# Reordering the written-out schedule of a mixture-of-experts and Mamba block on four engines

## The reference

```python
x = x + 0.5 * ffn(layernorm(x))        # 8 experts, hidden 512, top 2 of 8 by a softmax gate, silu
x = x + mixer(layernorm(x))            # two Mamba blocks in a row, the second followed by a chunked memory read
x = x + 0.5 * ffn(layernorm(x))        # the same expert weights again
```

## Time and profile before

| | us |
|---|---|
| median of 3 runs (1960.1 to 1960.5) | 1960.4 |
| the profiled execution's own time | 1957.77 |
| its span, first to last instruction | 1955.9 |
| VectorE busy | 1723.2 (88%) |
| TensorE busy | 1511.4 (77%) |
| ScalarE busy | 1142.5 (58%) |
| GpSimd busy | 755.6 (39%) |

### The profile page before, as it was taken

One profiled execution on the slowest core, in us unless ns is written; L12 is line 12 of the kernel. 1 busy time (PEld: TensorE's weight loads), 2 busy tenths in 40 slices (PEclk: granted clock), 3 DMA queues, 4 the chain that ended last, 5 costly groups with the idle time before them and its releaser, 6 DMA issues. The chain is left out here.

```text
span 1955.9 us, 26508 instructions
## 1 busy us (share of the span) xinstructions
PE 1511.4 (77%) x8672; PEld 1313.5 (67%) x8672; DVE 1723.2 (88%) x2421; ACT 1142.5 (58%) x2206; POOL 755.6 (39%) x366
## 2 busy tenths in 40 slices
PE   5778547878878787878888787887888888548778
PEld 4667435777767676767677667776777777437667
DVE  4269999999989998999989999899989999999941
ACT  3276555566756665656666566665755657436522
POOL 0005354444434354454325354353434454443310
PEclk9889767879989889998989898988889799668879
DMA  5000000000000000000000000000000000000000
GB/s 182 1 6 1 1 1 1 6 1 1 1 13 1 1 1 7 6 1 1 1 8 6 1 1 7 7 1 1 1 6 1 1 1 1 6 1 1 1 6 6
DMA packets 11688, 14.45 MB, mean 7 GB/s; under 512 B 400, under 2 KB 8592, under 8 KB 11408
## 3 DMA queue, kind: packets, MB, share of 16 engines
q1 hardware_dynamic: 11536, 12.56, 2.0%
HBM read 10.46 MB, written 2.10 MB: 6 GB/s over the span
## 5 line engine op out<-in xcount | busy, mean ns | idle before, releaser
L1101 POOL TENSOR_TENSOR acc<-acc,G 128x1024 f32<-128x1024 f32 x192 | 557.9, 2905 | 467.6 <-DVE G L922 461.4
L912 DVE TENSOR_TENSOR_SCAN hs<-dA,dbu 128x1024 f32<-128x1024 f32 x256 | 646.4, 2543 | 3.1 <-issue 2.2
L566 ACT ACTIVATE raw<-b_h 128x512 f32<-128x512 f32 x512 | 305.0, 598 | 340.7 <-PE b_h L328 324.8
L623 ACT ACTIVATE dA<-delta,A 128x255 f32<-128x255 f32 x1024 | 422.7, 495 | 55.3 <-DVE hs L912 35.8
L405 PE MATMUL b_r<-bcr,selr 128*128 128x256 f32 x1024 | 245.5, 343 | 199.8 <-DVE G L922 118.5
L405 PEld LDWEIGHTS b_r<-bcr,selr 128*128 128x128 f32 x1024 | 184.0, 217 | 249.3 <-DVE G L922 134.5
L922 DVE TENSOR_TENSOR G<-hs,b_r 128x1024 f32<-128x1024 f32 x256 | 309.9, 1211 | 9.6 <-issue 3.0
L902 DVE TENSOR_TENSOR dbu<-du,b_r 128x1024 f32<-128x1024 f32 x256 | 308.2, 1209 | 0.4
L326 PE MATMUL b_h<-xh,w1h 128*128 128x512 f32 x512 | 242.4, 473 | 83.7 <-DVE xa L838 27.9
L335 PE MATMUL b_h<-w2s,raw 128*128 128x128 f32 x2048 | 279.7, 292 | 0.0
L335 PEld LDWEIGHTS b_h<-w2s,raw 128*128 128x128 f32 x2048 | 269.3, 209 | 1.1
(11 more groups left out here) (144 smaller groups left out, 1652.8 us busy)
## 6 DMA issues: line engine op xcount, KB each, us to landing
xin<-x_dram SPq DMA_DIRECT2D x8, 256.0 KB, 2.9
raw<-w_dram SPq DMA_DIRECT2D x1, 2048.0 KB, 11.2
out_dram<-ob SPq DMA_DIRECT2D x8, 256.0 KB, 2.3
prm<-pack_dram SPq DMA_DIRECT2D x1, 1124.5 KB, 5.2
hs<-sel_dram SPq DMA_DIRECT2D x2, 512.0 KB, 12.4
G<-sel_dram SPq DMA_DIRECT2D x2, 512.0 KB, 7.6
dA<-early_dram SPq DMA_DIRECT2D x1, 512.0 KB, 11.5
dbu<-early_dram SPq DMA_DIRECT2D x1, 384.0 KB, 11.7
```

The lines of the kernel that those rows point to most:

```text
L566: do(hT[e % 2][:, c, :], H[i % 2][:, :], ACT.Silu).then_inc(f_hact, 1)
L623: last = do(dA[j % 4][:, d, k, 1:], delta[b][:, k, 1:], ACT.Exp, scale=A[:, k, s:s + 1])
L912: V.tensor_tensor_scan(flat(hs[j % 2]), flat(dA[j % 4]), flat(dbu[j % 2]), 0.0, ALU.mult, ALU.add)\
L1101: Q.tensor_tensor(acc[b][:, :, :, :], (G[0] if j == 1 else acc[b])[:, :, :, :], G[j % NG][:, :, :, :], ALU.add).then_inc(q_gs, 1)
```

## The change

The strings of `ORDER` are replaced by others; no other line is changed. The words of each string are the same as before but for two things that cross a slot's border: VectorE's f2 and f3 of the FFN in slots 2 and 3 move from slot 3 to slot 2, and two of TensorE's pieces move from slot 1 to slot 0 (33 and 31 pieces in place of 31 and 33; 24 and 40 in slots 2 and 3 stay).

```diff
@@ -44,39 +44,37 @@
 
 ORDER = {
     "tensor": (
-        "t0 t1 fturn in t2 fgate p2 t3 p2 t4 p5 t5 p2 t6 t7 xp p1 dt p2 t8 p1 t9 p2 t10 p3 m1 t11 p2 t12 "
-        "t13 p4 m2 p3 t14 m3 t15 p1 m4 p1",
-        "p2 t0 t1 t2 p5 out p6 turn t3 p1 t4 t5 in p2 t6 t7 p2 t8 t9 xp p1 t10 p2 t11 p1 t12 p1 dt p4 t13 "
-        "t14 p6 t15",
-        "t0 fturn t1 fgate p1 t2 p1 t3 out p4 t4 p5 turn t5 p2 t6 in t7 t8 p1 t9 p3 t10 xp p1 t11 p2 t12 p2 "
-        "t13 p2 dt t14 t15",
-        "p5 t0 p1 turng t1 p3 in t2 t3 t4 p8 t5 t6 xp p4 t7 t8 dt m1 p1 t9 t10 p3 t11 p1 m2 p2 t12 p2 t13 "
-        "t14 p2 m3 p5 t15 p3 m4"),
-
-
+        "t0 t1 t2 fturn in t3 fgate t4 p2 xp p4 t5 t6 p7 t7 dt t8 t9 p4 m1 t10 t11 p5 t12 p3 m2 p1 t13 p2 m3 p2 "
+        "t14 t15 p1 m4 p2",
+        "t0 p1 t1 p5 t2 p1 out t3 t4 p5 t5 turn t6 in p1 t7 p1 t8 p1 xp p1 t9 p1 dt t10 t11 p4 t12 p4 t13 p6 t14 "
+        "t15",
+        "fturn t0 t1 fgate p1 t2 t3 p3 out p5 t4 p2 t5 p2 turn t6 t7 in t8 p1 t9 p1 t10 p2 xp p1 t11 p4 dt p2 t12 "
+        "t13 t14 t15",
+        "p5 t0 p3 turng t1 p1 in p1 t2 p2 t3 t4 p4 xp p2 t5 t6 p1 t7 p1 dt p1 t8 p2 t9 p2 m1 t10 t11 t12 m2 p4 "
+        "t13 p4 t14 m3 p2 m4 p3 t15 p2",
+    ),
     "scalar": (
-        "d0 fhigh d1 d2 r xm F0 ftanh F1 d3 d4 proj d5 sp F2 F3 oT d6 v d7 rT",
-        "d0 d1 F4 F5 d2 turned d3 d4 d5 d6 r xm F6 proj F7 d7 sp",
-        "fhigh d0 d1 d2 F0 F1 ftanh d3 turned d4 d5 d6 d7 r xm F2 proj F3 sp",
-        "turned d0 d1 d2 F4 r xm F5 d3 proj d4 d5 d6 sp oT F6 v F7 rT d7"),
-
-
-
+        "d0 fhigh d1 d2 r xm F0 ftanh proj F1 d3 d4 d5 sp F2 oT F3 d6 v rT d7",
+        "d0 d1 F4 F5 d2 d3 turned d4 d5 d6 r xm d7 proj F6 F7 sp",
+        "d0 fhigh d1 d2 d3 F0 F1 d4 ftanh turned d5 d6 d7 r xm F2 proj F3 sp",
+        "d0 turned d1 d2 F4 r xm F5 proj d3 d4 d5 d6 d7 sp oT F6 F7 v rT",
+    ),
     "vector": (
-        "gate flow b0 flog ftop b1 s0 s1 g0 b2 g1 b3 s2 s3 fweights g2 b4 low f0 s4 f1 g3 b5 g4 s5 b6 g5 b7 "
-        "delta mask s6 g6 s7 g7 xb f2",
-        "f3 fstats gate b0 b1 s0 xsum s1 un g0 b2 g1 s2 f4 b3 fnorm s3 g2 f5 b4 g3 b5 s4 s5 g4 b6 g5 s6 b7 "
-        "low s7 g6 f6 f7 g7 delta",
-        "flow b0 flog gate s0 b1 g0 xsum ftop b2 un s1 s2 g1 b3 lx fweights s3 g2 b4 f0 g3 f1 s4 b5 g4 s5 "
-        "b6 g5 b7 s6 s7 ln low unx g6 delta g7",
-        "f2 b0 b1 f3 s0 gate g0 b2 s1 s2 fstats g1 b3 low g2 s3 b4 g3 f4 s4 f5 b5 g4 b6 delta mask s5 s6 g5 "
-        "b7 g6 s7 g7 f6 fnorm f7 xb"),
-
+        "b0 b1 gate flow s0 flog b2 ftop g0 s1 fweights s2 g1 b3 low g2 s3 f0 g3 b4 f1 b5 delta s4 s5 g4 b6 g5 "
+        "mask b7 f2 s6 s7 g6 g7 xb",
+        "f3 fstats b0 b1 gate s0 s1 xsum g0 g1 un b2 b3 f4 s2 s3 g2 b4 fnorm f5 g3 s4 b5 g4 s5 b6 g5 s6 b7 low f6 "
+        "delta s7 f7 g6 g7",
+        "flow b0 flog ftop b1 gate s0 s1 xsum g0 g1 b2 un b3 s2 s3 fweights g2 lx b4 g3 f0 f1 b5 s4 ln g4 s5 b6 "
+        "g5 b7 low unx s6 delta g6 s7 f2 g7 f3",
+        "b0 b1 s0 gate b2 g0 s1 s2 g1 low b3 g2 s3 g3 b4 b5 fstats f4 f5 s4 delta g4 s5 mask b6 g5 s6 b7 g6 s7 f6 "
+        "g7 fnorm xb f7",
+    ),
     "gpsimd": (
         "a1 a2 a3 a4 a5 a6 a7",
         "rms rs froot a1 a2 a3 a4 a5 a6 a7",
-        "rms a1 a2 rs lnx rmsx a3 a4 a5 a6 a7",
-        "a1 a2 a3 a4 froot a5 a6 a7"),
+        "rms rs a1 a2 lnx a3 rmsx a4 a5 a6 a7",
+        "a1 a2 a3 froot a4 a5 a6 a7",
+    ),
 }
```

## The result

The changed kernel takes **1828.0 us** (median of 4 runs, 1825.4 to 1829.5) against 1960.4 for the kernel before in the same comparison (1960.1 to 1961.6): ratio 0.932, 95% interval 0.931 to 0.934. The direction was right, the size was not. The profiled execution took 1825.4 us.

What follows compares the result with a forecast made beforehand. VectorE was taken as the bound; 11.6 us per group over six groups (69.6) plus 12 for groups 0 and 7 made 82 off 1957.8, giving 1876, and 1878 us as median. Range 1845 to 1930 us.

Steps and rivals of the forecast that it cites:

- The stock of 16.7 us per group: VectorE's time lost per group before the change, in scans, delta, du and xn held by GpSimd adds (meetings): 16.7 us.
- Meetings left, 7.2 per group: VectorE instructions still held by GpSimd adds in the new order: 0.1 + 2.0 + 2.6 + 2.5 us over four slots.
- The chain of fturn, in, fgate is as long as before, 9.3 us: Slot 0, TensorE: time from f7's end to the logits stays at 9.3 us.
- the wait that was to be 1.9: Slot 0: VectorE's wait for the logits shrinks from 4.9 to 1.9 us, 3.0 gained.
- TensorE's lateness, 1.8 per group: TensorE's B7 about 0.9 and f2 0.6 us late in slot 0, C7 0.3 in slot 3: 1.8 lost per group.
- Rival 1: TensorE falls behind in places, p6 10.9 us at half clock; gain 4 to 8 per group, about 1915 us; chance 0.21.
- rival 2: TensorE's clock falls through new waits and it becomes the bound, slower than before: 2050 us at worst; chance 0.09.
- Half the gain in groups 0 and 7: Groups 0 and 7, half their slots without FFN, gain half as much: 12 us for both.
- The cover of GpSimd's short steps: froot and rs move by one add on GpSimd; costed at nothing, the norm needing froot being ten words later.
- Rival 3: All meetings and waits go, TensorE never late: 14 to 15 us per group, about 1848 us; chance 0.08.

Runs made afterwards that it cites:

- before_filled_tensore: Kernel before, with two extra unused matmuls ahead of t0 and two ahead of fturn in TensorE's slot 0; 1954.7 us, ratio 0.995 to 0.998.
- after_old_gpsimd: Changed kernel with GpSimd's four old strings put back (rs, rmsx and froot differ in place, slots 2 and 3); 1839.8 us, against 1828.0.
- after_norms_moved_2: Changed kernel with VectorE's fnorm moved behind delta in slots 1 and 3, and slot 3 ending s7 g7 f6 xb f7; 1822.9 us, against 1828.0.

## Why the prediction was right in direction and wrong in size

**The mechanism holds.** VectorE bounds the kernel, its scans, delta, du and the words of the norms are held by GpSimd's adds, and how much is lost follows from the order. Small adds took 125 us from the kernel before with no order changed. The stock of 16.7 us per group was right within 1%.

**The bill by terms.** The forecast had 82 us, the spans differ by 132.4. From the runs with small adds, 92.7 of these are meetings (135.3 to 42.6): 71 in groups 1 to 6, where the forecast had 57, and 21 in groups 0 and 7, where it had about 10 of its 12. VectorE's rest fell by 29.5, where it had about 15; the waits for logits alone fell by 24.1 (40.5 to 16.4). The other 10.2 us of busy time (1587.9 to 1577.7) are in no term of the forecast; 3.3 of them are in un (10.9 to 7.6 with small adds) and 4.6 in inputs and products (618.7 to 614.1), the rest was not followed.

1. *Meetings left, 7.2 per group: too high.* A middle group has 5.2, by its busy time with full and with small adds: fnorm 1.2 in slot 1 and 2.1 in slot 3 (forecast 1.4 and 2.4), un 1.2 and unx 0.7 in slot 2 (1.4 and 0.9), un in slot 1 nothing (0.4), the scans 0.1 or less (0.7), du and delta none. So each norm word was high by 0.2 to 0.3, and the small meetings at s4 to s7 and at un in slot 1, counted by adding word to word from the slot's start, did not come. A scan directly behind a product goes first, and the add behind it waits; I had read that in rows 5 and still charged some of these.
2. *"The chain of fturn, in, fgate is as long as before, 9.3 us": wrong.* It takes 7.3 us in two groups, 8.2 in two and 9.2 in one, and the wait that was to be 1.9 is 0 to 1.8, 0.8 on average. I took durations from before for TensorE work that had run at the lower clock. before_filled_tensore shows the link of clock and length. Rows 7 held a sign of it: 3.69 us of idle ahead of fturn.
3. *TensorE's lateness, 1.8 per group: did not come.* In groups 2 to 5 inputs wait for spreads once per group, for 0.2 to 0.3 us; over the run it is 6.0 us, most of it in groups 0, 1 and 7, and the waits for expert sums (`ob` and `xa` for b_h, 19.4 before) are 18.4. I had let TensorE keep its old pace while VectorE got faster; its clock rose instead: it was 0.88 to 0.90 in the middle groups and is 0.93 to 0.95. Rival 1 stands on the same error, and rival 2 has the sign wrong. Rival 1's price was also read wrongly from rows 9: 16 matmuls of L335 are four downs and not two, so a down takes 0.49 or 0.91 us, and p6 takes 2.9 or 5.4 us, not 5.9 or 10.9.
4. *Half the gain in groups 0 and 7: too low.* By the ends of their last products they gained 9.4 us (with 1.6 from the start) and 15.1, 24.5 in place of 12. Groups 1 to 6 gained 108 in place of 69.6.
5. *The cover of GpSimd's short steps* was named only through the words that need their results. They also decide when adds run: 11.8 us in after_old_gpsimd.
6. *Rival 3 was added up wrongly*, and with it the low end. 14 to 15 per group is about the forecast without TensorE's lateness (11.6 + 1.8). "All meetings and waits go" is at least 16.7 + 3.9 = 20.6 by the prediction's own terms (3.9 are the waits that it had counted as gained, not all of them), 124 in six groups. With 12 for the others that is 1824. The range ended at 1845 because this sum was not made.

So the step that failed is the sum of what the new order leaves and gains: the meetings left, the chain's length, TensorE's lateness and groups 0 and 7 were each counted to the disadvantage of the gain. The direction was not luck. The range was missed because the four errors point one way and its low end left them out.

The slots of group 3 came out at 49.0, 51.1, 56.9 and 50.0 us where they had been 57, 55, 58 and 55: the gain is largest in slot 0, where the meetings and the wait for the logits both stood.

## What to carry to other kernels

When one engine's instructions are held by another's, as VectorE's by GpSimd's adds here, shrink the other's operand in an experiment: the fall in the first one's busy time is the whole stock of such losses, and an order can be judged by how much of it is left. A chain of TensorE work behind an idle stretch must not be costed at its old duration without reading off the granted clock that it ran at. Orders of several engines belong together: in slots 2 and 3 VectorE's new strings alone gave a fifth of the gain, TensorE's a loss, so price a word that moves on every queue that it passes, and add up the best case by the same terms as the forecast.

## What the runs showed of the hardware that was not expected

- The border of a hardware loop costs about 2 us on VectorE (1.89 to 2.03 in after_norms_moved_2) when its last words come directly before it, and shows on TensorE in the kernel before as well (2.04). On VectorE it is not seen where the last norm was held for 3.18 us and the words behind it waited for nothing, and taking that meeting away gained nothing (1818.0 and 1818.9).
- Four short norm instructions in a row are met by one add for 2.1 us in all (3.18 in place of 1.11), though each is done in 0.34 us alone: the add gets in between them. (The prediction had 2.4 for this.)
- Eight matmuls of 128x256 took 1.97 us after a pause of 1.44 us on TensorE and 3.69 after one of 2.23, but 3.76 after pauses of 2.04 and 1.05.
